# Attention's prologue: seven PSUM banks released by the operation that reads each, a second buffer of projected parts inside X, one semaphore per stacked head, and value projections between the pieces

## The reference, cut to what matters

```python
q = (x @ Wq.T + bq).reshape(b, l, 32, 16).transpose(0, 2, 1, 3)   # k, v alike
scores = einsum('bhqd,bhkd->bhqk', q, k) / sqrt(16)
scores = where(tril(ones(l, l)), scores, -inf)
out = einsum('bhqk,bhkd->bhqd', softmax(scores), v)
return out.transpose(0, 2, 1, 3).reshape(b, l, d) @ Wo.T + bo
```

## Time and profile before

| | us |
|---|---|
| median of 3 runs | 4203.76 |
| lowest and highest | 4201.26, 4205.95 |
| the profiled execution, its own time | 4211.65 |
| its span in the trace | 4209.6 |
| PE busy | 3867.7 (92%) |
| DVE busy | 2758.7 (66%) |
| ACT busy | 1705.1 (41%) |
| POOL busy | 1814.9 (43%) |

### The profile page before, as it was taken

One profiled execution on the slowest core, in us unless ns is written; L12 is line 12 of the kernel. 1 busy time (PEld: TensorE's weight loads), 2 busy tenths in 40 slices (PEclk: granted clock), 3 DMA queues, 4 the chain that ended last, 5 costly groups with the idle time before them and its releaser, 6 DMA issues.

```text
span 4209.6 us, 61612 instructions
## 1 busy us (share of the span) xinstructions
PE 3867.7 (92%) x18088; PEld 2818.5 (67%) x18088; DVE 2758.7 (66%) x5102; ACT 1705.1 (41%) x3555; POOL 1814.9 (43%) x1977
## 2 busy tenths in 40 slices
PE   6889899889999999989978998997999999999797
PEld 4444478567777777767754445885777777777676
DVE  3567455677777777764536673556777777777646
ACT  1344321355555555542213443113555545555412
POOL 1111334356556655543211114442665556655532
PEclk8687799999999999999976777998999999999999
DMA  3221011011100110002032210110111000100111
GB/s 74 56 37 32 30 47 46 20 38 29 33 20 25 35 33 27 25 1 80 23 75 56 38 30 29 54 39 25 34 33 30 28 25 25 35 28 23 36 53 35
DMA packets 84630, 151.95 MB, mean 36 GB/s; under 512 B 16488, under 2 KB 18616, under 8 KB 84432
## 3 DMA queue, kind: packets, MB, share of 16 engines
q1 hardware_dynamic: 82320, 145.38, 13.1%
q10 hardware_dynamic: 2112, 4.19, 0.3%
HBM read 119.37 MB, written 4.19 MB: 29 GB/s over the span
## 4 chain that ended last, share of the span: by engine, by line
PE 72%; issue 8%; DVE 8%; ACT 4%; DVEq 2%; POOL 2%; POOLq 1%; DMA 1%; SPq 1%; ACTq 1%; PEldq 0%; PEld 0%
PE banks L520 16%; PE banks L521 15%; PE banks L522 15%; PE banks L928 5%; PE banks L764 4%; PE banks L745 4%; PE banks L721 3%; PE banks L921 2%; DVE conv L1575 2%; PE banks L941 2%; DVEq L1578 1%; PE banks L863 1%; PE banks L864 1%; ACT conv L1128 1%; DVE conv L1572 1%
## 5 line engine op out<-in xcount | busy, mean ns | idle before, releaser
L1575 DVE SCALAR_TENSOR_TENSOR conv<-banks,cpar,conv 128x509 f32<-128x509 f32 (+2 forms) x576 | 428.6, 744 | 113.3 <-ACT conv L1128 98.2
L1094 ACT ACTIVATE probs<-banks 128x1024 f32<-128x1024 f32 (+3 forms) x384 | 298.8, 809 | 315.1 <-PE banks L745 313.7
L1908 POOL TENSOR_SCALAR_AFFINE_SELECT probs<-probs 128x256 f32<-128x256 f32 x256 | 104.0, 406 | 663.4 <-ACT probs L1094 663.0
L721 PE MATMUL banks<-stack_k,stack_q 48*128 48x512 f32 (+3 forms) x768 | 326.2, 495 | 60.6 <-DVEq L1467 20.0
L1355 DVE TENSOR_TENSOR Y<-banks,Y 128x512 f32<-128x512 f32 x368 | 253.2, 691 | 160.9 <-PE banks L522 159.5
L1973 POOL TENSOR_TENSOR state<-state,gt 128x512 f32<-128x512 f32 x112 | 134.1, 1197 | 507.6 <-PE banks L921 507.6
L520 PE MATMUL banks<-xhi,f_hi 128*128 128x512 f32 x800 | 324.4, 405 | 30.9 <-POOL f_lo L1778 16.6
L520 PE MATMUL banks<-xhi,wx_hi 128*128 128x512 f32 x768 | 314.2, 409 | 6.8 <-DVE conv L1575 6.6
L521 PE MATMUL banks<-xhi,f_lo 128*128 128x512 f32 x800 | 319.5, 399 | 0.0
L522 PE MATMUL banks<-xlo,f_hi 128*128 128x512 f32 x800 | 319.4, 399 | 0.0
L521 PE MATMUL banks<-xhi,wx_lo 128*128 128x512 f32 x768 | 308.2, 401 | 0.0
(11 more groups left out here) (217 smaller groups left out, 10174.5 us busy)
## 6 DMA issues: line engine op xcount, KB each, us to landing
m_raw<-in_w_mamba SPq DMA_DIRECT2D x224, 256.0 KB, 2.6
f_raw<-in_w_ffn SPq DMA_DIRECT2D x50, 768.0 KB, 4.6
stack_q<-part_hi SPq DMA_DIRECT2D x128, 64.0 KB, 2.5
stack_k<-part_hi SPq DMA_DIRECT2D x128, 64.0 KB, 2.5
x_next<-in_x SPq DMA_DIRECT2D x6, 1024.0 KB, 8.6
wqk_raw<-in_w_attn SPq DMA_DIRECT2D x8, 512.0 KB, 3.7
stack_q<-part_lo SPq DMA_DIRECT2D x64, 64.0 KB, 2.4
stack_k<-part_lo SPq DMA_DIRECT2D x64, 64.0 KB, 2.4
```

Of the source, the lines that this page charges most:

```text
L721: r = pe.matmul(dst[:, 0:cols], stack_q[buf][base:base + ROWS, h, i * P:(i + 1) * P], stack_k[buf][base:base + ROWS, h, s * HALF:s * HALF ...
L1094: act.activation(probs[n % 2][:, 2 * p:2 * p + 2, 0:w], banks[:, 2 * p:2 * p + 2, 0:w], ACT.Exp, scale=1.0 / HD ** 0.5).then_inc(exp_done[ ...
L1575: r = dve.scalar_tensor_tensor(out=rest, in0=src[:, 0:HALF - lag], scalar=cpar[:, o:o + 1], in1=rest, op0=ALU.mult, op1=ALU.add)
```

## The change

`ring_banks` gives every use of a bank its bank by name. Before the first score seven banks are in turn (4, 5, 7, 0, 1, 2, 3), from then on three. The use waits for the semaphore of the very operation that read the bank last: `part_lo_ready` for a projection, `mt_ready` for maxima, `ring_free` for the others. The drains behind `part_lo` and `mt_lo` are gone. The first score of each of the banks 0 to 3 waits for that bank's last reader of the prologue.

Entries are cut into what PE does and what the reader does: values_in and values_out, proj (two halves of six matmuls), proj_hi and proj_lo, maxima and maxima_out. The reader's entry can stand later in `ORDER`. The prologue has proj 0, two values, then 48 pieces with six values (at n = 3, 9, ... 33, read at n = 8, 14, ... 38) and two uses of proj 1 in halves (n = 36, 40, 43, 46). The other two uses of proj 1 are in quad 0, after its steps 1 and 3.

`part_hi` and `part_lo` have a second buffer for odd f, which lies in X. ACT waits for the previous row's output before it writes there. X is loaded at the end of attention, after all stacks. `stacked` is one semaphore per parity and head. SP's list has a new order. `STEPS` now holds tuples of keys with one key each, and `blocks` gives for each the same columns as before.

```diff
+                part_hi = [sb("part_hi", [P, 2, L], F32R, stack=s2)[:]]
+                part_lo = [sb("part_lo", [P, 2, L], F32R, stack=s2)[:]]
+                for part, h in ((part_hi, 0), (part_lo, 1)):
+                    own = X[:, h * CPH:(h + 1) * CPH, :].rearrange("p (w u) d -> p w (u d)", w=2)
+                    part.append(own.bitcast(F32R))
...
+        stacked = [[sem(f"stacked{par}_{h}") for h in range(QUAD)] for par in range(2)]
...
+        MAIN_BANKS, FIRST_BANKS = (4, 5, 7), (4, 5, 7, 0, 1, 2, 3)
+        PROJ_STEPS = {(0, 1): (1, 2), (0, 3): (1, 3)}
+        for t, f in ((1, 2), (3, 3)):
+            PROJ_STEPS.update({(t, 2 * use + 1): (f, use) for use in range(4)})
...
             for use in range(4):
-                yield "proj", 0, use
-            for i in range(5):
+                yield from project(0, use)
+            for i in range(2):
                 yield "values_in", i
+                yield "values_out", i
             for n in range(NP):
-                if n in (3, 9, 15):
-                    yield "values_in", 5 + (n - 3) // 6
-                if n in (21, 27, 33, 39):
-                    yield "proj", 1, (n - 21) // 6
-                yield "piece", 0, n
+                if n % 6 == 3 and n < 36:
+                    yield "values_in", 2 + n // 6
+                if n % 6 == 2 and 2 < n < 42:
+                    yield "values_out", 1 + n // 6
+                if n in (36, 40, 43, 46):
+                    yield "proj", 1, int(n > 40), int(n in (40, 46))
+                if n in (40, 46):
+                    yield "proj_hi", 1, int(n > 40)
+                if n == 45:
+                    yield "proj_lo", 1, 0
+                yield from some(1)
             yield "maxima", 0
-            for _ in range(AHEAD):
-                yield "piece", *pieces.pop(0)
+            yield from some(2)
+            yield "maxima_out", 0
+            yield from some(2)
+            yield "proj_lo", 1, 1
+            yield from some(AHEAD - 4)
...
-                    if t % 2 and n < 8 and n % 2 and (t + 3) // 2 < NQ // 2:
-                        yield "proj", (t + 3) // 2, n // 2
+                    if (t, n) in PROJ_STEPS:
+                        yield from project(*PROJ_STEPS[t, n])
...
+        def ring_banks():
+            last, bank_of, before = {}, {}, {}
+            for use in RING_USES:
+                started_at = ORDER.index(use)
+                main = started_at >= ORDER.index(("score", 0, 0, 0))
+                allowed = MAIN_BANKS if main else FIRST_BANKS
+                k = min(allowed, key=lambda i: (last[i][2] if i in last else -1))
+                bank_of[use[:3]], before[use[:3]] = k, last.get(k)
+                last[k] = release(use)
+                if not main:
+                    first_scores = dict(last)
+            return bank_of, before, first_scores
...
+                load_qk(1)
                 stack(0)
                 stack(1)
-                load_qk(1)
+                put_maxima(0)
+                load_qk(2)
                 held(sp, v_used, b + 1)
                 ones_in(1)
-                put_maxima(0)
-                for h in range(2):
-                    held(sp, out_done[h], START + b * 16)
-                    sp.dma_start(X[:, h * CPH:(h + 1) * CPH, :], x_half(b, h)).then_inc(x_kept[h], 16)
-                load_qk(2)
                 stack(2)
-                stack(3)
                 put_maxima(1)
-                put_maxima(2)
                 load_qk(3)
...
+                for t in range(2, NQ):
+                    if t + 1 < NQ:
+                        stack(t + 1)
                     put_maxima(t)
...
-                        if n == 0:
-                            pe.wait_ge(stacked[t % 2], (b * (NQ // 2) + t // 2 + 1) * STACKED)
-                        pe.wait_ge(ring_free, b * RING + ring - 2)
+                        if i == 0:
+                            pe.wait_ge(stacked[t % 2][h], (b * (NQ // 2) + t // 2 + 1) * STACKED)
+                        bank_free(BEFORE[use])
...
                                                  op0=ALU.add, op1=ALU.subtract).then_inc(part_lo_ready, 1)
-                        dve.drain().then_inc(ring_free, 1)
```

More of the change, by code:

```diff
@@ L289, in attention_order, with some, project @@
+        PROJ_STEPS = {(0, 1): (1, 2), (0, 3): (1, 3)}
+        for t, f in ((1, 2), (3, 3)):
+            PROJ_STEPS.update({(t, 2 * use + 1): (f, use) for use in range(4)})
         def attention_order():
+            pieces = [(t, n) for t in range(NQ) for n in range(NP)]
+            def some(count):
+                for _ in range(count):
+                    if pieces:
+                        yield "piece", *pieces.pop(0)
+            def project(f, use):
+                yield "proj", f, use, 0
+                yield "proj", f, use, 1
+                yield "proj_hi", f, use
+                yield "proj_lo", f, use
@@ L312, in attention_order @@
                             yield "maxima", t + 1
-                        for _ in range(0 if turning else 2 if n in (2, 3) and q == 0 else 1):
-                            if pieces:
-                                yield "piece", *pieces.pop(0)
+                            yield "maxima_out", t + 1
+                        yield from some(0 if turning else 2 if n in (2, 3) and q == 0 else 1)
                     if n > 0:
@@ L393, in stack @@
                                 sp.dma_start(dst[at:at + HD, h, :].bitcast(F32),
[L394 removed]
+                                             part[f % 2][src, which, :].bitcast(F32)).then_inc(stacked[par][h], 16)
                 def put_maxima(t):
@@ L439, in _ @@
                 sp.dma_start(bo_sb[:], bo).then_inc(wo_in, 16)
+                for par in range(2):
+                    for h in range(QUAD):
+                        held(sp, stacked[par][h], (b + 1) * (NQ // 2 * STACKED))
+                for h in range(2):
+                    sp.dma_start(X[:, h * CPH:(h + 1) * CPH, :], x_half(b, h)).then_inc(x_kept[h], 16)
                 leave(sp, b, ATT)
@@ L1068, in _ @@
                 enter(act, b, ATT)
-                ring = 0
                 for what, *arg in ORDER:
-                    if what == "proj":
+                    if what == "proj_hi":
                         f, use = arg
@@ L1076, in _ @@
                             act.wait_ge(wqk_in, (b * (NQ // 2) + f + 1) * 32)
[L1077 to L1085 removed]
+                        if use == 0 and f > 1:
+                            for par in range(2):
+                                for h in range(QUAD):
+                                    act.wait_ge(stacked[par][h], (b * (NQ // 2) + f - 1) * STACKED)
+                        if use == 0 and f == 1:
+                            for h in range(2):
+                                act.wait_ge(out_done[h], START + b * 16)
+                        act.wait_ge(ring_done, b * RING + RING_ENDS.index(("proj", f, use)) + 1)
+                        act.activation(part_hi[f % 2][:, which, s * HALF:(s + 1) * HALF], bank[RING_BANK["proj", f, use]],
+                                       ACT.Identity, bias=qk_b[:, f % 2, which:which + 1]).then_inc(part_hi_ready, 1)
                     elif what == "score" and arg[2] % 2:
                         t, n, p = arg[0], arg[1], arg[2] // 2
[L1088 to L1089 removed]
+                        w = sum(width for _, _, _, width in blocks(n))
                         it = b * (NQ * NS) + (t * NS + n)
@@ L1456, in _ @@
                 held(dve, mask_built, b + 1)
-                ring = 0
                 for what, *arg in ORDER:
-                    if what == "proj":
+                    if what == "proj_lo":
                         f, use = arg
```

222 lines of the change are left out of this document (107 added, 115 removed).

## The result

The changed kernel takes 4132.4 us, the median of 4 runs (4120.98 to 4139.81), against 4204.85 for the kernel before. The ratio is 0.9827, with a 95% interval of 0.9803 to 0.985. Two later rounds of the same two kernels gave 0.9831 (0.9807 to 0.9855) and 0.986 (0.9827 to 0.9894). In those later rounds the kernel before also spread widely: 4183 to 4237 us over 51 runs, its medians between 4205 and 4209. The forecast was 4147 us. The profiled execution took 4139.81 us, 71.8 less than that of before.

What follows compares the result with a forecast made beforehand. PE and DVE were taken to alternate in the prologue. Terms 11.5 + 27.5 - 10.0 + 1.0 and 11.5 + 24.7 - 10.0 + 1.0 save 57.2 us: 4154.4, scaled to 4147 us; 8-in-10 range 4122 to 4182.

Steps and rivals of the forecast that it cites:

- Step 1: Prologue, first piece: waiting for one stacked head instead of the whole stack brings it 11.5 us earlier in each row.
- Step 2: Prologue, first piece to first score: 42 us, bounded by PE, against 69.5 and 66.7; gains of 27.5 and 24.7 us.
- The tail: End of the prologue, last pieces to first score: 5.5 us before, 6.0 us forecast with the turned maxima read later.
- DVE's waits for V and `part_lo`: Sign in the prologue: DVE's waits for these fall from 32 to under 15 us.
- Step 3: Quad 0: two projections moved there from the prologue cost 5.0 us each, 10.0 us a row; bounds 2.8 and 7 each.
- The sign of 47 to 49 us: Sign in the quads: maxima of quads 0 and 1 come 47 to 49 us apart instead of 38.3.
- Step 4: Drains behind `part_lo` and `mt_lo` removed: gain of 1 us a row, ends 0 and 4.
- Step 5: SP's new order and X loaded at the end of attention: zero cost, with 12 us of slack for the stacks.
- at most 1 us was named as the sign: Sign at the first scores: they wait for `mt_lo` no more than 1 us.
- rival D: Quads: maxima queued on SP behind a whole stack delay first scores, up to 15.2 us each; 4253 us; chance 0.04.
- The clock: Sign in the prologue's middle: granted clock above 0.85, where rival B would show near 0.5.
- Rival B: Prologue stays at 1.2 GHz, 64 us from piece to score; 4191 us; chance 0.19 together with a half-way case.

Runs made afterwards that it cites:

- three_at_once: The changed kernel with three banks instead of seven in the prologue and each V read directly behind its projection: 4187.28 us, ratio 0.9955 to the kernel before.
- read_at_once: The changed kernel, still with seven banks, with each V of the prologue read directly behind its projection: 4141.71 us, ratio 0.9818 to the kernel before.
- heads_only: The kernel before with one semaphore per stacked head and nothing else of the change: 4205.33 us, ratio 0.9992.

## Why the prediction was right

The forecast was 57.2 us less; 71.8 were measured in the profiled executions and 72.5 between medians. The mechanism is the one named, and the four terms of the prologue came within 2.1 us each. The terms outside it did less well, and two of the signs that were named failed.

- Step 1, the first piece: 11.0 and 11.4 us for 11.5, with PE idle for 1.86 us (about 1.9 forecast). It was counted as a term of its own, but it is one only because the V projections moved behind it: alone on the kernel before it shortened the two prologues by 3.3 us, and nothing is left of it in the whole.
- Step 2, from first piece to first score: 44.0 and 44.1 us for 42. The cadence was 4.4 us, which is 3.9 plus 0.5 for the hand-over where 0.4 was taken. The tail from the end of the last pieces (88.4) to the score was 6.6 us for 6.0. The start at half clock isn't the rest of the difference: the first V projection took 4.5 us (51.62 to 56.13) instead of 3.0, less than the 2 us allowed for. The hand-overs make up most of it: the forecast counted eight of 0.4 us, but proj 1 goes in four halves, so there are ten, and at 0.5 us they make 5 us instead of 3.2. three_at_once and read_at_once show that four more banks are worth 18 to 22 us of the 25.5 and 22.6; the other 5 to 6 go with the rest of the change. DVE's waits for V and `part_lo` went from 32 us to none in the first row, where under 15 was named as the sign.
- Step 3, the moved projections: from first score to the last maxima +6.5 and +4.4 us with the drains' gain in it, for +9.0. Two projections in quad 0 cost 5.9 us in the first row (44.2 against 38.3) and 12.0 in the second (49.2 against 37.2), 3 to 6 each around the 5.0 of the forecast, whose rows showed quad 0 of the first row only. The sign of 47 to 49 us from the maxima of quad 0 to those of quad 1 was met in neither row. What made the sum smaller is quad 1, which was to stay as it was and came out 3.3 and 5.1 us shorter.
- Step 4, the drains: up to 0.42 us of DVE's time each, and 0.02 us more of a wait for PE where it was looked at, less than the 0.1 taken. The 1 us a row is neither confirmed nor contradicted by the whole, but with the drains back quads 0 and 1 are 5 to 6 us a row longer in the one trace than in five of the six rows without. That would also account for the shorter quad 1. If so, the term was too small, and what a drain costs lies in the quads and not in the wait behind `part_lo`; it isn't shown.
- Step 5, SP's order and X: a quad's first score waits 3.60 and 3.70 us for `mt_lo` in the two prologues, where at most 1 us was named as the sign. From the turned maxima to the score the prologue takes 5.1 us in the first row, where the kernel before took 4.1, and PE now has its six pieces done sooner, which makes the wait longer. In the quads behind it the whole wait for `mt_lo` is 0.2 us a row, so no stack stands before the maxima on SP, and rival D, and with it any slower outcome, is out. The stretch between the rows took 1630.5, 1631.7 and 1638.2 us in the three traces, for 1636.1.
- The clock: full from 58 us to 90 us in the prologue (0.53 in such a place before), 0.93 over the whole of it. Rival B is out. The rule of the Trainium skill, "TensorE: Matmul & The Clock Gate", section "A second HAM failure mode: psum-queue depth-cycling", puts a swinging clock down to the short pauses of a matmul stream that cycles through banks. The seven banks are cycled through without a pause of PE, and their clock doesn't swing (1.00); with three banks PE pauses (busy 2.66 of 4 us) and the clock swings (0.52, 0.91, 0.50).

The term that was missing is the clock of quad 7. It was taken as unchanged and gave -11.1 us in the first row and -0.1 in the second; the rest outside the quads gave -0.8. It is luck as far as the forecast goes, and can't be put down to one edit: the changed kernel's own three traces have it at 33.0 to 33.9 us four times and at 45.5 twice, the two rows of the kernel before at 45.0 and 45.6, and heads_only, which is as slow as that, at 40.7 twice. Without it the two executions differ by 60 us, for 57.2 forecast. What sets the clock of quad 7 is left open.

## What to carry to other kernels

Two engines that hand banks to each other work side by side only if the consumer's backlog is longer than the producer's longest piece of other work. That is the reading of the runs above, and to use it, count how many pieces the consumer can still read while the producer does something else, and give the ring that many banks; here three were too few and seven enough, and no number between was run. An earlier start is worth what the work behind it can take up, so test it together with that work and not alone: here it was worth 3 us of the two prologues alone and 24 us together with the rest. A stretch that stopped taking turns gained twice, by the idle time and by the clock (0.70 to 0.93). And a program whose times spread by 30 us needs more than four runs of both kernels: the first three runs of the kernel before lay within 5 us.

## What the runs showed that was not expected

- The same instructions in quad 7 take 33.0 to 33.9, 40.4 to 40.7 or 45.0 to 45.6 us, over all the runs that add nothing to it. At 45.5 the granted clock is 0.50 with PE busy 20.00 of 20 us; at 33.9 it is 1.00. So PE without a gap stayed at the lower of the two levels (1.2 of 2.4 GHz) in this stretch.
- Projections of 128x128x512 matmuls every 4.4 us, with 48-row pieces between, held 1.00 from 58 to 90 us in the first row.
- Quad 0 with one projection took 38.4 us in one row (mean clock 0.91), less than the 41.9 us without any (0.71). Less work doesn't by itself make a quad shorter, as its clock differs from trace to trace.
- With three banks, delaying the reader of one of them by five pieces cost 12 to 16 us a row; with seven banks the same delay cost 0.5 to 2.2 us in the prologue, and nothing that the times of the runs show.
- The kernel before spreads as widely as the changed one, 4183 to 4237 us.
